# One set of running sums a batch for both directions of a Mamba-2 layer, with new orders on every engine

## The reference

```python
zxbcdt = x @ Win                               # 256 -> 1160
z, xBC, dt = split(zxbcdt)                     # 512, 640, 8
xBC = silu(causal_conv4(xBC) + convb)          # xs 512, B 64, C 64
dt = softplus(dt + dtb); A = -exp(Alog); dA = exp(dt * A)
h = dA_t * h + dt_t * B_t x_t                  # 8 heads, step by step
y = C_t . h + D * xs
y = y * silu(z); y = y * rsqrt(mean(y*y)) * normw
out = concat(fwd, bwd) @ Wo + bo
```

## Time and profile before

| | |
|---|---|
| Time, median of 3 runs (range) | 601.73 us (599.51 to 604.13) |
| Profiled execution: its time, its span | 603.06 us, 601.3 us |
| Busy: PE, ACT, DVE, POOL | 577.1, 530.9, 476.6, 407.9 us |
| Mean granted clock of TensorE | 0.994 of full |
| Opening and first scan; seven turns; last scan and end | to 67 us; 67 to 558.7 us; to 601.3 us |

### The profile page before, as it was taken

The page is one execution under the profiler, slowest core; times in us unless marked ns, Lnnn a source line. Parts: engine busy times, 40 slices in busy tenths (PEclk is TensorE's granted clock), DMA queues, the critical chain, the costliest instruction groups (busy, mean ns, idle before and its releaser), DMA issues.

```text
span 601.3 us, 13719 instructions
## 1 busy us (share of the span) xinstructions
PE 577.1 (96%) x4320; PEld 464.5 (77%) x4320; DVE 476.6 (79%) x983; ACT 530.9 (88%) x1191; POOL 407.9 (68%) x427
## 2 busy tenths in 40 slices
PE   2998999999999999999999999999999999999996
PEld 1785788887888878887888878888788877888774
DVE  3689788986979779796889859797797968888663
ACT  4799998989989899998989899898999989898952
POOL 1016948797397965977487973979659774878932
PEclk9998999999999999999999999999999999999998
DMA  7464703436071621718034450717207180344601
GB/s 202 158 189 103 220 3 123 135 111 180 0 228 37 210 70 33 222 28 262 0 118 137 125 165 0 228 35 210 72 28 227 27 263 1 83 140 127 167 1 35
DMA packets 42009, 70.71 MB, mean 118 GB/s; under 512 B 6464, under 2 KB 29056, under 8 KB 41984
## 3 DMA queue, kind: packets, MB, share of 16 engines
q1 hardware_dynamic: 41984, 70.40, 39.4%
HBM read 59.37 MB, written 4.72 MB: 107 GB/s over the span
## 4 chain that ended last, share of the span: by engine, by line
PE 86%; ACT 6%; issue 3%; POOL 2%; DVE 1%; SPq 1%; DMA 1%; POOLq 0%; ACTq 0%; DVEq 0%
PE mi L612 18%; PE pj L478 12%; PE pj L479 10%; PE pj L480 10%; PE py L571 10%; PE py L589 4%; PE mi L678 4%; PE mi L558 4%; PE mi L538 3%; PE gm L545 1%; POOL xw L1856 1%; ACT L948 1%; PE mi L671 1%; PE mi L598 1%; PE mi L498 1%
## 5 line engine op out<-in xcount | busy, mean ns | idle before, releaser
L1372 DVE SCALAR_TENSOR_TENSOR xc<-pj,cw,xc 128x510 f32<-128x510 f32 (+2 forms) x240 | 173.4, 742 | 6.8 <-ACT xc L930 5.1
L963 ACT ACTIVATE bs<-bs,s_all 128x128 f32<-128x128 f32 x512 | 159.3, 391 | 0.0
L478 PE MATMUL pj<-xnt_hi,w_hi 128*128 128x512 f32 x288 | 128.0, 444 | 0.0
L1877 POOL TENSOR_TENSOR yg<-yg,sz 128x512 f32<-128x512 f32 x60 | 76.9, 1286 | 75.2 <-DVE yg L1418 75.2
L479 PE MATMUL pj<-xnt_lo,w_hi 128*128 128x512 f32 x288 | 114.6, 398 | 0.0
L480 PE MATMUL pj<-xnt_hi,w_lo 128*128 128x512 f32 x288 | 114.5, 398 | 0.0
L612 PE MATMUL mi<-wc,yg 128*128 128x256 f32 x480 | 111.8, 383 | 0.0
L612 PEld LDWEIGHTS mi<-wc,yg 128*128 128x128 f32 x480 | 88.8, 190 | 12.9 <-issue 1.8
L1856 POOL TENSOR_TENSOR xw<-xdt,w_end 128x512 f32<-128x512 f32 x48 | 49.4, 1043 | 54.6 <-ACT w_end L948 53.4
L1399 DVE TENSOR_TENSOR bs<-bs,gm 128x512 f32<-128x512 f32 x128 | 85.0, 675 | 0.2
L1384 DVE TENSOR_TENSOR xdt<-mi,dt 128x512 f32<-128x512 f32 x64 | 42.5, 686 | 45.4 <-PE mi L538 45.0
(11 more groups left out here) (152 smaller groups left out, 986.8 us busy)
## 6 DMA issues: line engine op xcount, KB each, us to landing
bs<-rows_dram SPq DMA_DIRECT2D x64, 512.0 KB, 5.4
es<-rows_dram SPq DMA_DIRECT2D x64, 192.0 KB, 4.8
cc<-bcm SPq DMA_DIRECT2D x32, 128.0 KB, 2.4
xres<-in_x SPq DMA_DIRECT2D x8, 512.0 KB, 3.6
out<-ot SPq DMA_DIRECT2D x32, 128.0 KB, 4.7
xin<-in_x SPq DMA_DIRECT2D x7, 512.0 KB, 3.6
cz<-bcm SPq DMA_DIRECT2D x16, 128.0 KB, 2.4
yg<-in_fwin SPq DMA_DIRECT2D x2, 320.0 KB, 3.4
```

What stands on the lines that cost most here:

```text
L478: pe.matmul(ps[:], hi(k), xnt_hi[:, k, :], start=(k == 0), stop=False)
L963: i = nc.scalar.activation(bs[:, h, Q * c:Q * c + Q], bs[:, h, Q * c:Q * c + Q], ACT.Relu, bias=s_all[:, d, 0, h, c:c + 1], scale=-1.0)
L1372: i = dve.scalar_tensor_tensor(xc[:, t, to], pj[bank][:, of], cw[:, d, t, KW - 1 - s:KW - s], xc[:, t, to], ALU.mult, ALU.add)
L1877: pool.tensor_tensor(yg[:, d, p, :], yg[:, d, p, :], sz[:, d, p, :], ALU.mult).then_inc(yg_ready, 1)
```

## The change

The two directions' sums are made together, once a batch. PE: two `tri` products and one product with `ones` over all 64 columns go to one bank, and one transposition of 128 columns gives S of both directions and, below them, 64 rows that are not used. DVE's `s_copy` empties the bank in one go for both directions (S into `s_all`, total minus S into `wd`, totals into `s_ends`). ACT makes one row copy, one row exp, one `w_end` and one `e_end` a batch. SP stores the rows of both directions with one DMA and their exps with one DMA. Since S of the next batch now overwrites `s_all` while the reversed scan still needs its own, ACT keeps the reversed direction's S in `s_late`. The stores wait until all loads of the previous batch have landed. The tables of small banks shrink to 23, 36 and 13 uses. The lists of all engines are written in another order; those of the two places that the prediction uses most stand below.

```diff
-LOOP = ["1x0", "1x1", "1bt", "1x2", "1x3", "a0", "a1", "1s0", "1s1", "dtm", "dtt", "0ss", "0o0", "1s2", "0S", "0o1",
-        "0ST", "0x0", ..., "1S", "1ST", "t0", "t1", "f0", "f1", "t2", "t3", "f2", "f3"]
+LOOP = ["1x0", "1x1", "1x2", "1x3", "1bt", "a0", "a1", "1s0", "1s1", "dtm", "dtt", "0ss", "0o0", "1s2", "S", "0o1",
+        "ST", "0bt", "0x0", ..., "t0", "t1", "f0", "f1", "t2", "t3", "f2", "f3"]
...
# SP
+            def put_rows(phase, it, b):
...
+                        sp.wait_ge(bs_loaded[p], 16 * 2 * b)
...
+                sp.dma_start(rows_dram[0].rearrange("d h (c q) -> (d h c) q", c=NC), s_rows[:, 0, :]).then_inc(rows_stored, 16)
# PE
+            def sums(phase, it, b):
+                for d in range(2):
+                    pe.matmul(ps[:, NCH * d:NCH * d + NCH], tri[d], al[:, d].rearrange("p c h -> p (c h)"), start=(d == 0), stop=True,
+                              skip_group_check=True)
+                pe.matmul(ps[:, 2 * NCH:4 * NCH], ones, al[:].rearrange("p d c h -> p (d c h)"), start=False, stop=True,
+                          skip_group_check=True).then_inc(full, 1)
+            def s_transposed(phase, it, b):
+                pe.wait_ge(s_ready, b + 1)
...
+                pe.transpose(ps[:, 0:Q], s_all[:].rearrange("p i d h c -> p (i d h c)"), ident).then_inc(full, 1)
# PE, forward_scan: sums(phase, it, b, 1) and s_transposed(phase, it, b, 1) are gone from between mix, intra
-                intra(b, 0, 0)
                 state(phase, it, b, 0, 2)
+                intra(b, 0, 0)
                 intra(b, 0, 1)
# ACT
+            def late_sums(b):
+                act.wait_ge(s_ready, b + 1)
+                nc.scalar.activation(s_late[:], s_all[:, 0, 1], ACT.Copy).then_inc(late_ready, 1)
+            def decay_w(phase, it):
+                bank, used = misc_use(phase, it, "S")
+                act.wait_ge(mi_free[bank], used + 2)
+                nc.scalar.activation(w_end[:], wd[:], ACT.Exp).then_inc(w_ready, 1)
# DVE
+            def s_copy(phase, it, b):
+                dve.tensor_copy(sums, ps[:, 0:2 * NCH].rearrange("p (d c h) -> p d c h", d=2, c=NC)).then_inc(s_ready, 1)
+                dve.wait_ge(s_ready, b + 1)
+                dve.tensor_tensor(wd[:]..., ps[:, 2 * NCH:4 * NCH]..., sums, ALU.subtract)
+                for half in range(2):
+                    i = dve.tensor_copy(s_ends[LANES[half]]..., ends)
+                i.then_inc(free, 1)
# SP, opening
+                load_consts()
+                load_small(0)
+                load_small(1)
+                load_win(0, 1, 0)
+                load_win(0, 1, 1)
                 load_dt()
```

More of the change, by code:

```diff
@@ L706, in reversed_scan @@
                 inter(phase, it, b, 1, 0)
+                project(nxt, 0, 3)
+                sums(phase, it, nxt)
+                mix(phase, it, b, 0, 2)
+                s_transposed(phase, it, nxt)
                 project(nxt, 0, 4)
-                sums(phase, it, nxt, 0)
-                mix(phase, it, b, 0, 2)
                 mix(phase, it, b, 0, 3)
-                project(nxt, 0, 5)
-                s_transposed(phase, it, nxt, 0)
                 intra(b, 1, 2)
@@ L715, in reversed_scan @@
                 inter(phase, it, b, 1, 1)
+                project(nxt, 0, 5)
                 project(nxt, 0, 6)
@@ L745, in first_scan @@
                 inter(phase, it, b, 0, 1)
+                project(b, 1, 6)
                 project(b, 1, 7)
@@ L836, in opening @@
                 project(0, 0, 2)
+                project(0, 0, 3)
                 fold(0)
@@ L944, in gate, with decay_e @@
                 nc.scalar.activation(sz[:, d, t - NCONV, :], pj[bank][:], ACT.Silu).then_inc(pj_free[bank], 1)
[L946 to L954 removed]
+            def decay_w(phase, it):
+                bank, used = misc_use(phase, it, "S")
+                act.wait_ge(mi_free[bank], used + 2)
+                nc.scalar.activation(w_end[:], wd[:], ACT.Exp).then_inc(w_ready, 1)
+            def decay_e(phase, it):
+                bank, used = misc_use(phase, it, "S")
+                act.wait_ge(mi_free[bank], used + 2)
+                nc.scalar.activation(e_end[:], s_ends[:], ACT.Exp).then_inc(end_ready, 1)
             def bound(b, d, h):
@@ L958, in bound @@
                 if h == 0:
-                    act.wait_ge(wd_ready, u + 1)
+                    act.wait_ge(late_ready if d else s_ready, b + 1)
+                upto = s_late if d else s_all[:, 0, 0]
                 act.wait_ge(bs_loaded[h // 2], 16 * (u + 1))
@@ L1526, in reversed_scan @@
+                mix(phase, it, b, 0, 0)
                 soft_rq(nxt)
+                state(phase, it, b, 1, 2)
                 soft_base(nxt)
                 soft_ratio(nxt)
-                state(phase, it, b, 1, 2)
                 soft_log1p(nxt)
-                mix(phase, it, b, 0, 0)
+                conv(nxt, 0, 1, 2)
                 dt_value(nxt)
+                mix(phase, it, b, 0, 1)
                 dt_decay(nxt)
-                mix(phase, it, b, 0, 1)
                 dt_floor(nxt)
+                weights(phase, it, b, 1, 4)
@@ L1684, in forward_scan @@
                 if ahead:
-                    norm1_aggr(b + 1, 0)
+                    norm1_aggr(b + 1, 3)
+                mix(phase, it, last, 1, 1)
+                conv(b, 1, 1, 2)
                 state(phase, it, b, 0, 2)
+                weights(phase, it, b, 0, 4)
+                conv(b, 1, 1, 3)
                 norm2_bn(phase, it, last, 0)
-                mix(phase, it, last, 1, 1)
-                weights(phase, it, b, 0, 4)
                 outputs(b, 0, 0)
+                weights(phase, it, b, 0, 5)
+                conv(b, 1, 0, 3)
                 norm2_bn(phase, it, last, 1)
```

588 lines of the change are left out of this document (275 added, 313 removed).

## The result

Over 13 runs of each, the changed kernel takes 599.22 us in the median (594.44 to 600.75), the kernel before 602.86 (599.51 to 604.26). The ratio is 0.993, with a 95% interval of 0.990 to 0.996. It is faster, by 3.6 us, in my range and of the sign forecast, but 10.3 us was forecast. By the prediction's own bounds (faster means under 595.7 us) this is "same", which had a chance of 0.26, and it is the number of rival B (599.1 us, chance 0.07). The profiled execution took 600.75 us (span 598.9), that of the kernel before 603.06.

A forecast was written before the change was run, and what follows sets the result against it. PE was taken to bound the kernel, its clock full outside the opening. Terms 4.0 + 2.1 + 1.4 + 1.2 + 1.6 = 10.3 us, from the profiled 603.06 to 592.8 us; range 588.5 to 600.5.

The forecast's parts named there:

- same: Whole kernel: median neither under 595.7 us (faster) nor over 607.7 (slower); chance 0.26.
- rival B: Whole kernel: only the removed work shows, the reordering gives as much as it takes; 599.1 us, chance 0.07.
- part 1: Sums and transposition on PE: less work, net 0.5 us in each of seven turns and the opening, 4.0 us.
- Part 2: Start of the reversed scan: an old `w_end` lets the projection come 0.3 us sooner, seven times, 2.1 us.
- Part 3: Forward scan: fewer cuts between `intra`, 1.4 us, bounds 0 and 3.5; fewer ACT table loads worth nothing by themselves.
- part 4: Opening and first scan: start worth nothing, first scan ends 1.2 us earlier, bounds -1.5 and 3.
- Part 5: Last scan: 1.2 us through the last `inter`, 0.4 from an earlier `last_norm(0)`; together 1.6 us, bounds 0 and 2.
- The opening's eighth share: Opening: the removed PE work gains 0.5 us there, as in each of the seven turns.
- the walk: Hand walk of the new lists through the old trace's spacings, handshakes of about 0.1 us left out or rounded.
- All that is stretched here, 1.4: Start of the reversed scan: upper bound of the gain there, 1.4 us a turn or 9.8.
- C: Head of the forward scan: ACT stands for the rows' round trip, slower, 610.3 us; chance 0.08.
- A: Both scans: DVE runs one step late and PE waits on it, about 0.8 us a turn, 598.4 us; chance 0.20.

The follow-up runs named there:

- 3: Kernel before plus idle matmuls, results unread, in PE's waits of the first scan (6 and 1) and the end (4 and 10): 599.66 us, ratio 0.995.
- kernel 4: Changed kernel plus idle matmuls, results unread, in PE's waits of the first scan (3 and 4) and the end (4 and 10): 595.39 us, ratio 0.989.
- kernel 12: kernel 1 plus idle matmuls and one unread 16-column exponential behind ACT's copy of B in the reversed scan: 597.34 us.
- kernel 1: Kernel before with sums, transposition, rows, exponentials and stores made once a batch, all orders, rings and queues as before: 605.32 us, ratio 1.004.
- 5: kernel 1 plus idle matmuls; on ACT, Relus of heads 0 and 1 first in the reversed scan, dt's bias ahead of the second decay: 605.86 us.
- 9: kernel 1 plus idle matmuls; ACT makes first convolution step and dt's bias ahead of head 1's Relus and exponential in the reversed scan: 607.02 us.
- 2: Changed kernel with DVE making only a quarter of x tokens 2 and 3 of the reversed scans (results wrong): 595.74 us.
- kernel 6: kernel 4 with x tokens 2 and 3 of the reversed scans in the two output banks, not the ring of two: 590.86 us, ratio 0.981.
- kernel 8: kernel 4 with the last scan put back in its old orders on five engines: 597.04 us.
- 11: kernel 6 with the opening and first scan in the orders of before, sums still merged: 591.09 us.

## Why the prediction was wrong

At full clock (kernels 3 and 4, turns and stages as above) the five terms stand so:

| term | forecast | measured | from |
|---|---|---|---|
| 1 less work on PE | 4.0 | 4.0 | 7 x 0.57, kernel 12 |
| 2 start of the reversed scan | 2.1 | 0 | 7.79 for 7.77 us |
| 3 fewer cuts | 1.4 | 0.3 to 0.6 | 7 x 0.04 to 0.08, kernel 12 against 4 and the changed one |
| 4 opening | 1.2 | -0.6 | 45.46 for 44.88 us from the seventh projection matmul on, part 1's share in it |
| 5 last scan | 1.6 | 0.15 | -0.2 to the last `inter`, +0.35 behind |

The terms add up to 3.9 to 4.2 us, for 4.3 of the medians. The spans to the end of the first scan (65.63 for 65.72 us) hide the loss of part 4, since the slow stretch was 0.7 us shorter in the execution of kernel 4.

**Rival B had it nearly right, and in part by luck.** It said that only the removed work shows and that the reordering gives as much as it takes: 599.1 us for the 599.22 measured, and 4.0 us from the removed work, as in the first row. But the old orders lose that work again (kernel 1), so the new ones do more than B had them do, and the plain kernels' 3.6 us has the clock in it.

**Part 1 was right for the turns.** The forward scan became 0.85 us shorter for 0.69, the reversed one 0.26 longer for 0.19. The opening's eighth share (0.5 us) is not to be seen: behind the slow stretch the first scan ends after 44.9 us with merging (5, 9, 12) and without it (3).

**Part 2 is the step that failed first.** I forecast 2.1 us and got nothing. I named the next bound rightly, the ring of two banks that DVE empties, and DVE's low parts were done at 6.86 us for the 6.85 of the walk. The error is in the last two handshakes. My walk let the second `state` start 0.05 us behind DVE's end; the row has 0.35 (212.91 to 213.26). PE's chain from B to the projection is 4.05 us of blocks and waits, where I had 3.85, and B itself was 0.14 later. That is 0.34, all of the gain. The wait I saw removed was 0.23 us long in the earlier trace rows, and a wait of 0.23 us stands there now. It was put down to POOL, but a second releaser stood beside it. DVE in the kernel before:

```profile
213.02 1.44 DVE L1297 TENSOR_TENSOR xnt_lo<-mi,xnt_hi 128x512 fp32r<-128x512 f32 x2 [0.63 <-ACT xnt_hi L894]
```

The low parts end at 214.46, and PE's second `state` starts 0.34 us later. The same 0.34 us lies there in kernels 1, 2, 6 and the changed one, where POOL is done long before. So without POOL's product the wait would have ended at the same time, as it does in kernel 1. "All that is stretched here, 1.4" was no waiting time but PE's own spacing. What there was to win, 0.63 us, kernel 6 won by banks.

**Part 3.** The forward scan's new order brought nothing: 33.31 us in kernel 1, 33.30 in the changed one with B's 0.44 counted. The 0.5 us that my walk was short may have been rounded handshakes, as I suspected and then took 0.2 of; no run splits them.

**What part 3 missed about ACT's loads.** It said that fewer loads are worth nothing. I counted the loads (eight to six) and not their places. One of those removed was free in a wait, and its table was used by what followed. Without new orders the change is slower, which no rival of mine had: C put the slower side at the row's round trip, and no wait of ACT for `rows_dram` is in the trace. Nor did A come: there is no wait of PE for `xc`.

**Part 4 had the wrong sign.** Forecast were 1.2 us beyond part 1's 0.5; the new orders of opening and first scan cost 0.5. From dt's transposition on, the merged kernels take 46.8 us in the old orders (5, 9, 12) and 47.3 in the new (4, 6, 8). The walk followed PE and DVE and took ACT's and POOL's products as soon as they were issued. `intra` indeed moved, but in the first scan two states wait 0.81 and 1.06 us and an `intra` 1.22 where before one waited 1.65 and one 0.42.

**Part 5.** `last_norm(0)` ahead of the third residual gave its 0.4 (0.34: from the last mixes to the first transposition 13.12 us for 13.46, kernels 4 and 3). The 1.2 us through the last `inter` were not there against the kernel before: 19.95 us for 19.78. PE bounds that one, as the prediction itself computed (18.6 of 19.8) and did not heed. What the new orders won (0.75 us for kernel 8's 20.70), merging had cost first.

**The rest** is the clock at the end: 4.3 us between kernels 3 and 4, against 3.6 between the plain ones. I did not look at it, since the earlier trace rows showed one dip in either half.

**The load's price.** The prediction took 1.28 us and no drain from the earlier trace rows, where the Trainium skill (ScalarE: Activation LUTs, What ACT_TABLE_LOAD costs) has a drain of 1.38 us more. Kernel 12 agrees with the row: load at 207.27, exponential at 208.56, 1.29 us later.

**Left open:** why the half clock takes the same mixes in some executions and spares them in others, of one kernel too (11 and 12); when the slow stretch of the opening ends, and whether the orders have a part in it; and what makes the merged last scan slow in its old orders.

## What to carry to other kernels

Before an operation is taken out, look at what it does for its neighbours. A table load that falls into a wait is free; when it is gone, the work behind it may have to load for itself, in time that is not free. In a stretch where one engine is busy from end to end, a removed wait of 0.2 us is worth little (the 0.44 us that kernel 6 removed made 0.67 a turn), and a walk with handshakes of 0.05 us is not fit to find it; take each release from a row (here 0.18 to 0.35 us from DVE's end to PE). Where the profile names one releaser of a wait, look whether another is done at nearly the same time. When merged work makes a kernel only a little faster, split the change into the merging and the order, and try the first by itself.

## What the runs showed of the hardware

- Idle matmuls in PE's waits (7 and 14 of 0.23 us in the kernel before) made both kernels faster by 3.3 and 3.8 us, and the granted clock then stayed at 1.00 (2.4 GHz) in the profiled executions. In the changed kernel without them it fell to 0.50 (1.2 GHz) at 52 us, behind waits of 0.81 and 1.06 us, and at 581 us, behind one of 0.96.
- Without an edit, the changed kernel's runs spread from 594.4 us at a mean clock of 1.000 to 600.8 at 0.989.
- After DVE's last read of a bank, PE's next matmul into it starts 0.18 us later (B at 209.79 behind x token 2's product, some 209.61) to 0.35 us (the second `state` at 213.26 behind 212.91).
- In the first 20 us PE's matmuls of 512 columns follow each other by 0.43 us and later by 0.23, though the windows say clock 1.00 for both. It ends at 17.5 us in the changed kernel and at 19.7 in the one before, and from dt's transposition to the seventh projection matmul behind it that makes 1.85 and 2.55 us.
